# A selective state-space kernel: the ScalarE's side work is cut into one PSUM read per job, put between the two halves of a step's exponentials, and seven whole-row operations beside it

## What is computed

```
h, gate = adaln(x, cond)                       # normalise, scale, shift
for fwd, and for bwd on the flipped sequence:
    xs, z = split(h @ in_w);  xs = silu(xs)    # 512 channels each
    proj  = xs @ xproj_w
    dt    = softplus(proj[:512] + dt_bias);  B, C = proj[512:576], proj[576:640]
    state = state * exp(dt * A) + (dt * xs) * B      # 512 channels x 64 states, over 256 steps
    y     = sum(state * C) + xs * D;  out = (y * silu(z)) @ out_w
x = x + gate * (fwd + bwd);  then an MLP with silu(h @ w1) * (h @ w2) @ w3
```

## Time and profile before

| | us |
|---|---|
| median of 3 runs | 5269.31 (5267.03 to 5272.09) |
| profiled execution, its own time | 5272.58 |
| its span | 5270.9 |
| busy in the span: PE, DVE, ACT, POOL | 4869.9, 4721.3, 3384.6, 3754.7 |
| the 2048 scans (L894), busy | 4536.0 |
| mean granted TensorE clock | 0.989 |

### The profile page before, as it was taken

The page is one execution under the profiler, slowest core; times in us unless marked ns, Lnnn a source line. Parts: engine busy times, 40 slices in busy tenths (PEclk is TensorE's granted clock), DMA queues, the critical chain, the costliest instruction groups (busy, mean ns, idle before and its releaser), DMA issues. The chain is left out here.

```text
span 5270.9 us, 130492 instructions
## 1 busy us (share of the span) xinstructions
PE 4869.9 (92%) x44784; PEld 2658.3 (50%) x44784; DVE 4721.3 (90%) x2419; ACT 3384.6 (64%) x11498; POOL 3754.7 (71%) x6613
## 2 busy tenths in 40 slices
PE   6999999999999999999999999999999999776898
PEld 4555555555555555555555555555555555443444
DVE  2999999999999999999999999999999999996443
ACT  4767767676766766676766767676676767663112
POOL 4787878777787878777787878687887878674211
PEclk8999999999999999999999999999999999998999
DMA  3121211112121211112121211111121211113442
GB/s 107 39 65 45 65 38 54 56 39 62 43 61 44 66 41 50 56 40 62 43 61 43 67 40 52 55 45 56 43 61 43 64 40 46 31 29 111 145 153 68
DMA packets 433144, 306.75 MB, mean 58 GB/s; under 512 B 215920, under 2 KB 336240, under 8 KB 432496
## 3 DMA queue, kind: packets, MB, share of 16 engines
q1 hardware_dynamic: 428272, 294.39, 18.7%
q10 hardware_dynamic: 4224, 4.19, 0.2%
HBM read 187.27 MB, written 111.15 MB: 57 GB/s over the span
## 5 line engine op out<-in xcount | busy, mean ns | idle before, releaser
L894 DVE TENSOR_TENSOR_SCAN b_hs<-b_dA,b_u 128x1024 f32<-128x1024 f32 x2048 | 4536.0, 2270 | 184.5 <-ACT b_u L821 155.5
L1057 PE MATMUL b_ex<-b_dd,b_aw 32*128 32x512 f32 x8192 | 2751.5, 641 | 17.6 <-POOL b_dd L542 15.6
L1044 PE MATMUL b_u<-b_ud,b_bw 32*128 32x256 f32 x16384 | 2320.1, 400 | 276.9 <-DVE b_hs L894 255.9
L803 ACT ACTIVATE b_dA<-b_ex 128x496 f32<-128x496 f32 x4096 | 2303.5, 593 | 166.0 <-PE b_ex L1057 127.5
L1044 PEld LDWEIGHTS b_u<-b_ud,b_bw 32*128 32x128 f32 x16384 | 1417.5, 184 | 1122.7 <-issue 558.1
L821 ACT ACTIVATE b_u<-b_hin 128x32 f32<-128x32 f32 x1792 | 368.8, 206 | 1236.8 <-PE b_u L1044 1045.4
L542 POOL TENSOR_TENSOR b_dd<-b_dr,b_mask 128x512 f32<-128x512 f32 x1024 | 1074.9, 1050 | 51.5 <-DVE b_hs L894 39.8
L1076 PE MATMUL b_y<-b_hs,b_cw 128*32 128x256 f32 x16384 | 1104.8, 385 | 1.7 <-DVE b_hs L894 1.7
L551 POOL TENSOR_TENSOR b_ud<-b_ur,b_mask 128x512 f32<-128x512 f32 x1024 | 1085.6, 1060 | 0.0
L1057 PEld LDWEIGHTS b_ex<-b_dd,b_aw 32*128 32x128 f32 x8192 | 865.4, 183 | 62.0 <-ACT b_dA L803 35.7
L1076 PEld LDWEIGHTS b_y<-b_hs,b_cw 128*32 128x32 f32 x16384 | 426.9, 108 | 846.2 <-issue 663.3
(11 more groups left out here) (104 smaller groups left out, 2351.0 us busy)
## 6 DMA issues: line engine op xcount, KB each, us to landing
b_u<-scratch_ut SPq DMA_DIRECT2D x256, 128.0 KB, 2.9
scratch_y<-b_ysb SPq DMA_DIRECT2D x128, 256.0 KB, 2.1
scratch_xs<-b_xs SPq DMA_DIRECT2D x64, 256.0 KB, 2.5
scratch_sz<-b_sd SPq DMA_DIRECT2D x64, 256.0 KB, 2.2
scratch_dt<-b_sd SPq DMA_DIRECT2D x64, 256.0 KB, 2.1
scratch_ut<-b_uT SPq DMA_DIRECT2D x64, 256.0 KB, 2.6
b_ur<-scratch_ut SPq DMA_DIRECT2D x1024, 16.0 KB
b_dr<-scratch_dt SPq DMA_DIRECT2D x1024, 16.0 KB, 1.7
```

The costliest lines, as they stand in the source:

```text
L803: nc.scalar.activation(dA[:, j % NDA, h, :, 1:TC], src[:, :, 1:TC], ACT.Exp).then_inc(exp_done, 1)
L894: nc.vector.tensor_tensor_scan(hs[:, v, :, :, kp].rearrange("p d t -> p (d t)"), dA[:, j % NDA, :, :, :].rearrange("p h d t -> p (h d t)") ...
L1044: ins = nc.tensor.matmul(dst[:, :, tb, :], bw[row(r), c % 2, tb, :], ud[row(r), j // 2 % NPR, tb, :, :], start=(tb == 0), stop=(tb == NTB ...
L1057: nc.tensor.matmul(e[bank_of[what]][:, :], aw[row(r), p % DIRS, v, :, :].rearrange("p b s -> p (b s)"), dd[row(r), (p * PAIRS + j // 2) % ...
```

## The change

ACT's side work is split into two generators. `readers` takes each job with one instruction (Copy, or Identity with the bias) and is advanced between `decay(j+2)` of half 0 and of half 1; `works` does what is left on whole rows of 512 (Tanh, plus one, Abs, Exp, plus one, Ln, Relu) and is advanced at the end of the step as before. POOL's products come three steps later. Some jobs of `bc` and `ut` start at other steps. `share_banks` stays as it is.

```diff
-        UT_JOB = (18, 22, 23, 26)
+        UT_JOB = (18, 22, 23, 28)
...
-        BC_SLOT, BC_SPAN = (32, 48), 3
-        UT_SLOT, UT_SPAN = (64, 80, 82, 96), (2, 2, 1, 1)
+        BC_SLOT, BC_SPAN = (34, 50), 3
+        UT_SLOT, UT_SPAN = (64, 80, 84, 102), (2, 1, 1, 1)
...
                 def unit(q):
+                    yield from wait_steps(3)
...
                 def take_xz(q, i, b):
...
-                    nc.scalar.activation(dst[:, cols], job_bank(n)[:, 0:SEQ], ACT.Copy, scale=0.5)
-                    if m >= 2:
-                        act.wait_ge(silu_made, m - 1)
-                    nc.scalar.activation(th[:, i % 2, cols], job_bank(n)[:, 0:SEQ], ACT.Tanh, scale=0.5).then_inc(freed, 1)
+                    nc.scalar.activation(dst[:, b * SEQ:(b + 1) * SEQ], job_bank(n)[:, 0:SEQ], ACT.Copy, scale=0.5
+                                         ).then_inc(freed, 1)
+
+                def bend(q, i):
+                    m = q * SILUS + i
+                    src = xs[:, i, :] if i < JB else sd[:, i - JB, :]
+                    act.wait_ge(freed, first_job(q) + XZ_JOB[i] + CB)
+                    if m >= 2:
+                        act.wait_ge(silu_made, m - 1)
+                    nc.scalar.activation(th[:, i % 2, :], src, ACT.Tanh).then_inc(bent_up, 1)
...
                 def take_dt(q, j, b):
-                    nc.scalar.activation(pre[:, m % 2, cols], job_bank(n)[:, 0:SEQ], ACT.Relu, bias=bias)
-                    nc.scalar.activation(ey[:, cols], job_bank(n)[:, 0:SEQ], ACT.Abs, bias=bias).then_inc(freed, 1)
+                    nc.scalar.activation(pre[:, m % 2, b * SEQ:(b + 1) * SEQ], job_bank(n)[:, 0:SEQ], ACT.Identity,
+                                         bias=dtb[:, q % DIRS, j:j + 1]).then_inc(freed, 1)
...
                 def log_part(q, j):
+                    nc.scalar.activation(ey[:, :], pre[:, m % 2, :], ACT.Abs).then_inc(bent, 1)
+                    yield
...
+                    yield
+                    nc.scalar.activation(pre[:, m % 2, :], pre[:, m % 2, :], ACT.Relu).then_inc(relued, 1)
...
+                def works(q):
+                    nc.scalar.preload_act_table_set("exp_and_others")
+                    yield from wait_steps(3)
+                    for i in range(JB + 1):
+                        bend(q, i)
+                        yield from wait_steps(2)
+                        plus_one(q, i)
+                        yield from wait_steps(2)
+                    nc.scalar.preload_act_table_set("natural_log_exp_and_others")
+                    yield from wait_steps(6)
...
-                def one_pass(p, last, side):
+                def one_pass(p, last, reads, work):
                     for j in range(JP):
...
-                        if j + 2 < JP:
-                            decay(p, j + 2)
-                        elif not last:
-                            decay(p + 1, j + 2 - JP)
+                        if then:
+                            decay(*then, 0)
+                        next(reads, None)
+                        if then:
+                            decay(*then, 1)
                         if j % HALF == 0 and half >= 2:
                             read_y(half - 2)
-                        next(side, None)
+                        next(work, None)
```

More of the change, by code:

```diff
@@ L178, in main_phase @@
         bent = sem("b_bent")
+        relued = sem("b_relued")
         logged = sem("b_logged")
@@ L721, in take_bt, with readers @@
                     last.then_inc(freed, 1)
[L723 to L726, removed]
+                def readers(q):
                     for i in range(JB + 1):
[L728 to L734, removed]
+                        for b in range(CB):
+                            take_xz(q, i, b)
+                            yield from wait_steps(2)
+                    yield from wait_steps(4)
                     for j in range(JB):
-                        yield from wait_steps(2)
                         take_dt(q, j, 0)
@@ L764, in unit @@
                         take_xz(q, i, 1)
-                        yield
+                        if i == JB + 1:
+                            yield from wait_steps(10)
+                        elif i == JB + 2:
+                            yield from wait_steps(2)
+                            take_ut(q, 3)
+                            yield from wait_steps(2)
+                        else:
+                            yield from wait_steps(6)
+                    if q % DIRS == 1 and q + 1 < PASSES:
+                        for k in range(MB):
+                            yield from modulate(q // DIRS + 1, k)
+                            yield from wait_steps(2)
@@ L786, in _ @@
                         pass
-                for _ in unit(0):
-                    pass
+                reads, work = readers(0), works(0)
+                for _ in range(JP):
+                    next(reads, None)
+                    next(work, None)
                 act.wait_ge(a_loaded, 16 * RT * DIRS * CB)
@@ L821, in put_carry @@
                     nc.scalar.activation(u[:, j % 2, :, 0:H:TC], hin[:, j % NM, :, :], ACT.Copy).then_inc(carried, 1)
[L823 removed]
+                def one_pass(p, last, reads, work):
                     for j in range(JP):
                         half = (p * JP + j) // HALF
+                        then = (p, j + 2) if j + 2 < JP else None if last else (p + 1, j + 2 - JP)
                         if j >= STEPS:
                             put_carry(p, j)
[L828 to L831 removed]
+                        if then:
+                            decay(*then, 0)
+                        next(reads, None)
+                        if then:
+                            decay(*then, 1)
                         if j % HALF == 0 and half >= 2:
                             read_y(half - 2)
[L834 to L837 removed]
+                        next(work, None)
+                for j in range(2):
+                    for h in range(2):
+                        decay(0, j, h)
                 for p in range(PASSES):
[L839 removed]
+                    more = p + 1 < PASSES
+                    one_pass(p, not more, readers(p + 1) if more else wait_steps(0), works(p + 1) if more else wait_steps(0))
                 read_y(HALVES - 2)
```

113 lines of the change are left out of this document (63 added, 50 removed).

## The result

The changed kernel takes 5515.71 us (median of three executions, 5513.23 the fastest) against 5269.14 of the kernel before on the same chip: 1.0467 times as long, interval 1.0446 to 1.0487. A fourth execution (6972 us, at a granted clock of 0.65) is left out. The forecast was 5485, in a range of 5340 to 5560. The profiled execution took 5516.68 us; its span is 5515.0, 244.1 more than before.

The account below looks back on a forecast made before the run. Wherever a job holds a bank, the end of ACT's second `b_dA` sets PE's next pair of steps. Per pass 19.0 - 1.5 - 2.2 - 0.7 = 14.6 us, 219 for 15 passes, less 3 at the start: about 5485 us, range 5340 to 5560.

Parts of the forecast that it names:

- The forecast for `xz`: Reads between ACT's halves: delay 0.56, cycle 5.28 in later chunks; delay 0.73 in the first chunk, 5.8 us for 8 reads.
- slack: Spare time before a scan hides part of an isolated cycle's cost: 0.7 us a pass, once, in the first chunk.
- `dt`: ACT's reads with a bias, placed between the halves: delay 0.66 each, 5.3 us for 8 reads a pass.
- ut: ACT's Copy reads between the halves: 0.51 each, no wait for the job; four make 2.0 us a pass.
- `bt`: ACT's read between the halves: 0.3 us a pass, an estimate of half.
- the turn jobs: Jobs in every second unit, already holding their bank over two steps with two long reads each: no change.
- Tables and POOL: Gains a pass: 1.5 us from table loads on steps 23 and 85, 2.2 from POOL's products three steps later.
- the whole rows: Whole-row works at ACT's end of step: cost nothing, hidden in the wait for PE of 1.25 before each carry.
- the read finds its job ready: Rival: PE is ahead, so only the read's own length, 0.26 or 0.36, delays the second half; 5350 us; chance 0.1.
- POOL did stand idle: Rival: POOL becomes late too, waiting for the second `b_first`; 24 products a pass pass on 0.3, about 5590 us; chance 0.08.
- The hidden delay: Rival: PE's second exponent does not need the bank at once, so only gains stay; 5211 us, faster; chance 0.09.
- Ahead of the first scan: In unit(0), a whole-row Abs of 0.63 replaces four reads of 1.60, three times: -2.9 us.

Follow-up runs that it names:

- the changed booking: Changed kernel with the second half's bank noted free 0.1 step later and the turn jobs booked for two steps instead of one: 5283.06 us.
- the one with the read at the end: Changed kernel with the job's read again behind both halves of the exponentials: 5214.17 us; repeated on another chip, 5215.23 us.
- the run with both: Kernel before with POOL's products three steps later and the two table loads moved, nothing else: 5213.98 us.
- the moved product alone: Kernel before with only POOL's products for softplus and silu moved, as in the changed kernel: 5231.68 us.
- The last runs: Kernel before with POOL's products and table loads moved, 5213.98 us; on the same chip, changed kernel with its read behind both halves, 5215.23 us.
- the tables alone: Kernel before with only the table loads moved, for Ln to step 21, for Exp and Tanh to step 85: 5262.11 us.
- the kernel with the booking alone: Changed kernel with only the second half's bank noted free at 1.25 instead of 1.15 steps: 5334.95 us.

## Why the prediction was right, point by point

**The bound.** "When the second `b_dA` ends decides when the next pair of steps can begin" held at every place I looked, and more exactly than I put it. From the inject of an odd step to its `add_up` PE needs 1.05 us from the start of the second exponent on: it started 0.54 after the inject and the block took 1.59 with the changed booking, and 1.10 and 2.15 in the changed kernel (1710.66, 1711.76, 1712.81). The exponent starts 0.05 behind the read that empties its bank, and the delay goes in full into the cycle.

**The sizes.** The forecast for `xz` was a delay of 0.56 and a cycle of 5.28; measured are 0.57 after the carry and 5.30. The costs of the place are the changed kernel less the one with the read at the end, us late a pass:

```
reads of                forecast           measured
xz, first chunk (8)     5.8 - 0.7 slack      5.7
xz, later (8)           4.5                  4.3
bc (2)                  1.1                  1.2
dt (8)                  5.3                  5.9
ut (4)                  2.0                  1.9
bt                      0.3                  0.6
turn                    0                    0.3
sum                     18.3                 19.9
```

Mis-sized by 0.6 each were `dt` (0.66 a read, measured 0.65 to 0.86, the most at step 40) and the slack of the first chunk, which was not there: its 5.8 counts nearly in full. `bt` was guessed at half its cost, and the turn jobs at nothing.

**The gains in a pass.** Tables and POOL stood at 3.7; the run with both gave 4.1, and the kernel with the read at the end is 3.6 below before. Inside, two errors cancel by luck: tables 1.5 forecast and 1.0 measured, POOL 2.2 and 3.0. At step 108 the moved product alone gave back 0.70, of which I took 0.2; in the changed kernel a part returns at 106, since the raised tanh comes later there. POOL's waits for `b_wy` went from 202.5 to 8.8.

**Works at no cost, one read at no gain.** I costed the whole rows at nothing, because ACT waited for PE there anyway, and took nothing for the second read and the halves saved. The last runs bear this out: 5213.98 without them, 5215.23 with them. ACT was busy 64% of the span before: the engine was not saturated. The Trainium skill's rule for fewer and larger operations (Perfetto Trace Analysis, Optimizing Scalar/DVE Operations) has saturation as its condition; it was not met here, and the gain did not come.

**The order of the queue.** ACT stood idle 0.19 us until the read at 1710.77, and the second half, which at the same point of the kernel before went ahead of the job's read, stood behind it; by the Trainium skill (PSUM — Partial Sum Buffer, Engine vs sequencer instructions) ScalarE's queue is strictly first in, first out, and the trace agrees.

**The rivals.** That the read finds its job ready did not happen in the changed kernel; it did when the read came a step later, at 5231. POOL did stand idle 863.3 us before `b_hm` instead of 443.5 (850.5 and 421.9 of it for `b_first`), but passed nothing on where I looked: ACT's idle time for POOL ahead of the carries fell from 182.9 to 141.4 us, and at step 18 the bank explains the cycle's growth in full. The hidden delay is out by the booking: only when the second exponent stopped needing that bank did the delay cost little.

**The sum.** Forecast +14.6 a pass, measured +16.2 (19.9 - 3.6): of 28 us that the profiled execution lies above the forecast's 5488.6, 25 are this. Ahead of the first scan it was -5.6 instead of -2.9; the tables alone moved that scan by 1.4, whole rows and single reads the rest. 5.9 us came behind the last scan, which the change doesn't touch and for which the forecast had nothing. From the start of the last scan to the end the kernels here take between 452 and 462 us with the same instructions, the changed one 462, with a mean granted clock of 0.94 in the last 375 us, the one before 456, with 0.96 in the last 369. I take it for scatter of the clock; no run was made for it. These two errors, -2.7 and +5.9, partly cancel, and that is luck too. A pass takes 311.7 us instead of 295.4, where 310 was forecast.

## What to carry to other kernels

A read placed ahead of an instruction is to be priced by what waits behind it in the queue, and by who waits for that: here 0.57 us a read, 300 us in all, for an instruction of 0.4 us. When the order of reads of a shared pool of banks is changed, the table that says when each bank comes free must be changed with it; two numbers there were worth 234 us. Here it was better still to leave the read where it was: 5214 us against 5283. And test each part of a change that has several: the part in its name (one read a job, whole rows) brought nothing measurable, two small moves of other work brought 60 us.

## What the runs showed of the hardware that I had not expected

An instruction that reads PSUM holds up the next one's start on ACT by less than its own length, and by little if nothing has to be waited for: 0.28 us for a Copy of 0.38 (1710.77 to 1711.05), 0.37 for an Identity with bias of 0.47 (step 28 of the changed kernel, 1735.20 to 1735.57). PE's exponents and injects, products of 32 rows each, overlap so far that the second exponent may start from 0.27 us (first chunk, read at the end: inject 1583.69, second `b_dA` ended 1583.91, `add_up` 1585.02) to 1.10 us behind the inject, and the `add_up` starts 1.05 us behind that start each time: in these blocks the time from inject to `add_up` is set by that start, though PE shows as busy all through. So PE at 93% busy is no proof that it is PE's own work that takes the time; with later starts its busy time grew from 4869.9 to 5134.4 us for the same 44784 instructions.

A wait on PE can also cost more than its length: behind the 2.31 us at step 113 of the kernel with the booking alone the granted clock was at its lower level, 0.50 (1.2 GHz), for some 2 us. In the changed kernel it was 1.00 from 200 to 5040 us.
